# New places for the steps of a pipelined two-attention transformer on one Trainium2 core

## The reference

```
x = x + attn_a(layernorm(x))     # 16 heads of 16, window |i-j| <= 32 and 4 global tokens, biases
x = x + ffn(layernorm(x))        # silu(x wg) * (x wu) wd, 256 -> 768 -> 256, int32 weights / 127
x = x + attn_b(layernorm(x))     # rotated q, k; num = exp(q_rot k_rot), den = sum(exp(q k)), causal
x = x + ffn(layernorm(x))        # the same weights as before
```

## Time and profile before

| | us |
|---|---|
| median of 3 runs | 2082.86 (2078.55 to 2094.81) |
| the profiled execution | 2086.18 |
| its span | 2084.1 |
| mean granted clock of TensorE | 0.939 |

### The profile page before, as it was taken

One profiled execution on the slowest core, in us unless ns is written; L12 is line 12 of the kernel. 1 busy time (PEld: TensorE's weight loads), 2 busy tenths in 40 slices (PEclk: granted clock), 3 DMA queues, 4 the chain that ended last, 5 costly groups with the idle time before them and its releaser, 6 DMA issues.

```text
span 2084.1 us, 63373 instructions
## 1 busy us (share of the span) xinstructions
PE 1814.1 (87%) x25221; PEld 1137.5 (55%) x25221; DVE 1423.0 (68%) x2978; ACT 1436.6 (69%) x3591; POOL 789.0 (38%) x1140
## 2 busy tenths in 40 slices
PE   5577889999898999989899998989899998988785
PEld 3353556555564655556465555646555565655444
DVE  6373768677676867767686776768687676865634
ACT  2227777786867777686777768676776867677591
POOL 0513243433434343342434334243434424343431
PEclk7687999999999999999999999999999999998987
DMA  6223344243434424343442424343243435333321
GB/s 155 72 44 94 81 118 102 91 109 86 119 76 117 108 84 110 89 112 74 117 108 84 113 87 113 73 132 93 85 113 90 113 69 135 90 102 86 79 70 37
DMA packets 129204, 199.51 MB, mean 96 GB/s; under 512 B 26720, under 2 KB 60512, under 8 KB 128880
## 3 DMA queue, kind: packets, MB, share of 16 engines
q1 hardware_dynamic: 128912, 195.44, 37.1%
HBM read 67.87 MB, written 51.52 MB: 57 GB/s over the span
## 4 chain that ended last, share of the span: by engine, by line
PE 45%; ACT 20%; SPq 11%; DVE 9%; DMA 7%; issue 4%; POOL 3%; POOLq 0%; ACTq 0%; DVEq 0%
PE psum L1120 10%; SPq L634 8%; ACT psum L1236 8%; PE psum L1150 5%; ACT probs_B L1226 4%; PE psum L1138 4%; PE psum L1071 4%; PE psum L1017 4%; DMA pack_b<-src_b 4%; PE psum L1053 3%; SPq L667 3%; PE psum L1094 3%; ACT probs_A L1219 3%; PE psum L883 3%; PE psum L1084 3%
## 5 line engine op out<-in xcount | busy, mean ns | idle before, releaser
L1236 ACT ACTIVATE psum<-psum 128x512 f32<-128x512 f32 x1024 | 607.6, 604 | 118.0 <-PE psum L1017 116.5
L1659 POOL TENSOR_TENSOR h<-tmp,h 128x512 f16<-128x512 f32 x192 | 227.7, 1186 | 410.7 <-DVE h L1540 410.7
L1226 ACT ACTIVATE probs_B<-psum 128x512 f32<-128x512 f32 x640 | 333.3, 632 | 51.0 <-PE psum L1038 48.7
L1017 PE MATMUL psum<-pack_b 48*128 48x512 f16 x1024 | 181.7, 396 | 53.2 <-DMA pack_b<-src_b 31.9
L1120 PE MATMUL psum<-xT,w_g 128*128 128x256 f16 x1536 | 204.0, 276 | 13.4 <-ACT psum L1236 12.1
L1265 ACT ACTIVATE tmp<-psum 128x512 f32<-128x512 f32 x192 | 118.2, 616 | 138.4 <-PE psum L1120 125.7
L1676 POOL TENSOR_SCALAR_AFFINE_SELECT probs_B<-probs_B 128x256 f32<-128x256 f32 x512 | 194.0, 412 | 50.4 <-ACT probs_B L1226 50.4
L1236 ACT ACTIVATION_READ_ACCUMULATOR psum<-psum 128x1 f32 x1024 | 209.6, 205 | 0.0
L1120 PE MATMUL psum<-xT,w_u 128*128 128x256 f16 x1536 | 208.7, 276 | 0.0
L1138 PE MATMUL psum<-w_d,h 128*128 128x256 bf16 x1536 | 200.8, 274 | 8.3 <-POOL h L1659 7.1
L1523 DVE SCALAR_TENSOR_TENSOR tmp<-tmp,psum 128x512 f32<-128x512 f32 x192 | 130.2, 679 | 96.3 <-ACT tmp L1265 95.8
(11 more groups left out here) (150 smaller groups left out, 3210.5 us busy)
## 6 DMA issues: line engine op xcount, KB each, us to landing
pack_b<-src_b SPq DMA_DIRECT2D x768, 64.0 KB, 2.4
pack_a<-src_a SPq DMA_DIRECT2D x384, 64.0 KB, 2.3
x<-in_L_attn_a_x_dram SPq DMA_DIRECT2D x32, 512.0 KB, 4.2
o_scr_A<-o_raw SPq DMA_DIRECT2D x64, 256.0 KB, 2.5
o_scr_B<-o_raw SPq DMA_DIRECT2D x64, 256.0 KB, 2.4
xn<-o_scr_A SPq DMA_DIRECT2D x32, 256.0 KB
rden_on<-r_scr_A SPq DMA_DIRECT2D x32, 256.0 KB
x_scr<-x SPq DMA_DIRECT2D x16, 512.0 KB, 2.8
```

Of the source, the lines that this page charges most:

```text
L1017: pe.matmul(score_bank("DP", n, q, e)[:, :], pack_b[r, j % 2, 0, 0, tile, t * P:(t + 1) * P], pack_b[r, j % 2, 0, 1, tile, :], start=True, ...
L1226: act.activation(probs["B"][:, i, :], score_bank("NP", n // 2, q, n % 2)[:, :], ACT.Exp, scale=SM_SCALE / W_SCALE ** 2)\
L1236: act.activation(bank[:, :], bank[:, :], ACT.Exp, scale=SM_SCALE / W_SCALE ** 2, accum_out=den[:, 0, j, 2 * tile + e, t:t + 1]).then_inc(d ...
L1659: pool.tensor_tensor(h[1][:, i % 2, :], tmp[:, i % 2, :], h[0][:, i % 2, :], ALU.subtract)\
```

## The change

The table `AT` has other places, for nearly all of its steps; nothing else in the kernel is changed. No step is added, removed or cut otherwise, `TURN` stays 425, and the rule for the banks is the same code, which gives other banks for the other order. A place is now given to a hundredth. Most steps keep their neighbours. Those whose order changes on their engine, as far as the text speaks of them (a place minus a multiple of 425 gives the order within a turn):

```
-    "A2": (545.8, 551.7, 553.1, 557.2, 558, 585.3, 587.2, 621.2, 628.3),
+    "A2": (546.52, 548.28, 548.95, 549.16, 563.1, 582.22, 590.11, 617.03, 619.36),
-    "MM": (505.5,),
-    "TM": (528.9,),
-    "TC": (531.4,),
-    "MX": (533.4,),
+    "MM": (496.94,),
+    "TM": (509.76,),
+    "TC": (518.06,),
+    "MX": (435.36,),
-    "AT": (576.4, 623.7, 656.2, 677.7),
+    "AT": (582.57, 625.43, 655.69, 677.7),
-    "DP": (1052.2, 1060.5, 1065.8, 1067.3, 1074.8, 1080.7, 1085, 1090.9, 1093.8, 1112.3, 1124.1, 1125.2, 1134.4,
+    "DP": (1055.22, 1055.45, 1059.54, 1059.55, 1069.69, 1071.13, 1083.56, 1089.05, 1089.06, 1111.48, 1121.99,
...
-    "DE": (1057.1, 1066.7, 1070.3, 1074, 1080.6, 1084.2, 1087.8, 1092.4, 1096, 1115.3, 1126, 1129.7, 1135.9, 1141.9,
+    "DE": (1053.5, 1064.4, 1065.39, 1074.89, 1076.27, 1077.72, 1083.02, 1089.83, 1095.82, 1120.72, 1125.56, 1126.72,
...
-    "NE": (1102.1, 1104.9, 1107.8, 1118.9, 1121.8, 1153.4, 1158.4, 1162.3, 1168.9, 1219.3, 1307.6, 1311.6, 1318.8,
+    "NE": (1099.96, 1100.14, 1103.85, 1104, 1119.45, 1152.13, 1152.27, 1162.22, 1165.78, 1206.07, 1307.09, 1311.67,
...
-    "UL": (1035.3, 1058, 1106.2, 1222.7),
-    "RL": (1083.5, 1119.4, 1139, 1277),
-    "VB": (1054.5, 1061.5),
+    "UL": (1027.19, 1054.99, 1101.57, 1218.45),
+    "RL": (1056.62, 1109.32, 1128.13, 1277.55),
+    "VB": (1057.97, 1067.28),
-    "GL": (425.1,),
-    "SL": (361.2, 384.2, 395.8, 407.3),
+    "GL": (435.68,),
+    "SL": (381.05, 382.82, 385.25, 385.26),
-    "W": (1030.1, 1039.1, 1046.2, 1053.2),
-    "W1": (1036.6, 1041.4, 1050.5, 1055.3),
-    "W2": (1043, 1052.7, 1062.3, 1077.6),
+    "W": (1031.74, 1039.53, 1050.63, 1054.55),
+    "W1": (1032.7, 1039.42, 1050.96, 1054.89),
+    "W2": (1045.95, 1047.35, 1058.22, 1067.07),
-    "PBT2": (1020.8, 1024.9, 1028.9, 1033),
+    "PBT2": (1020.8, 1028.33, 1028.34, 1033.43),
-    "F1FD": (922.2, 948.2, 955, 965.1, 979.8, 985.8),
+    "F1FD": (922.22, 950.59, 954.04, 965.06, 977.17, 980.21),
```

More of the change, by code:

```diff
@@ L64 @@
 AT = {
[37 rows of a table removed]
[L102 to L105, removed]
-    "GL": (425.1,),
-    "SL": (361.2, 384.2, 395.8, 407.3),
-    "GB": (361.2,),
-    "W": (1030.1, 1039.1, 1046.2, 1053.2),
-    "W1": (1036.6, 1041.4, 1050.5, 1055.3),
-    "W2": (1043, 1052.7, 1062.3, 1077.6),
[L112 to L116, removed]
@@ L117 @@
-    "PBT2": (1020.8, 1024.9, 1028.9, 1033),
[L118 to L163, removed]
-    "F1X1": (898.9,),
[L165 to L172, removed]
@@ L173 @@
-    "F1J": (916.7, 933, 946.1, 953.2, 965.6, 973.8),
-    "F1JL": (918.2, 934.6, 947.6, 954.7, 967.2, 975.3),
-    "F1FD": (922.2, 948.2, 955, 965.1, 979.8, 985.8),
[L176 to L189, removed]
[37 rows of a table added]
+    "VBC": (1064.43, 1086.91),
+    "VA": (362.08, 390.23),
+    "VAC": (363.66, 391.38),
+    "GW": (419.32,),
+    "GL": (435.68,),
+    "SL": (381.05, 382.82, 385.25, 385.26),
+    "GB": (361.17,),
@@ new lines @@
+    "W": (1031.74, 1039.53, 1050.63, 1054.55),
+    "W1": (1032.7, 1039.42, 1050.96, 1054.89),
+    "W2": (1045.95, 1047.35, 1058.22, 1067.07),
+    "PAT": (329.19, 335.99, 340.68, 341.4),
+    "PAT1": (326.69, 343.97, 350.19, 350.69),
+    "PAT2": (334.37, 346.37, 354.24, 354.85),
+    "PBT": (1020.89, 1020.9, 1021.84, 1024.96),
+    "PBT1": (1009.38, 1009.39, 1014.21, 1022.05),
+    "PBT2": (1020.8, 1028.33, 1028.34, 1033.43),
+    "OAOR": (764.01,),
+    "OAOL": (740.64, 742.56),
+    "OAOM": (784.38, 785.17),
@@ new lines @@
+    "OAOH": (788.67, 811.98),
+    "OAOW": (811.19, 818.14),
+    "OAO": (834.24, 844.65),
+    "OAOX": (834.2, 843.29),
+    "OBOR": (1445.53,),
+    "OBOL": (1450.55, 1472.59),
+    "OBOM": (1466.95, 1490.31),
+    "OBOH": (1469.95, 1493.14),
+    "OBOW": (1476.04, 1498.47),
+    "OBO": (1506.04, 1512.17),
+    "OBOX": (1514.72, 1516.81),
+    "F2L0": (1518.94,),
+    "F2L1": (1519.78,),
+    "F2L2": (1528.16,),
+    "F2L3": (1528.6,),
+    "F2L4": (1529.9,),
+    "F2L5": (1530.14,),
+    "F1L0": (856.41,),
@@ new lines @@
+    "F1L1": (858.81,),
+    "F1L2": (875.41,),
+    "F1L3": (879.96,),
+    "F1L4": (880.09,),
+    "F1L5": (881.36,),
+    "PBL0": (992.38,),
+    "PBL1": (993.27,),
+    "PBL2": (1001.55,),
+    "PBL3": (1002.19,),
+    "PBL4": (1003.04,),
+    "PBL5": (1003.44,),
+    "NAL0": (257.16,),
+    "NAL1": (263.89,),
+    "NAL2": (281.28,),
+    "NAL3": (282.21,),
+    "NAL4": (282.75,),
+    "NAL5": (289.13,),
+    "PAX": (310.79,),
+    "PAXH": (305.1,),
+    "PAX1": (310.5,),
+    "F2X": (1532.2,),
@@ new lines @@
+    "F2XH": (1529.11,),
+    "F2X1": (1534.18,),
+    "F1X": (895.27,),
+    "F1XH": (896.84,),
+    "F1X1": (898.9,),
+    "PBX": (1005.54,),
+    "PBXH": (1004.91,),
+    "PBX1": (1011.99,),
+    "F1G": (906.49, 920.92, 921.44, 943.43, 947.46, 962.98),
+    "F1GT": (904.09, 922.67, 924.36, 940.75, 943.07, 962.76),
+    "F1U": (906.5, 922.86, 940.35, 945.47, 959.61, 967.78),
+    "F1H": (906.96, 923.61, 926.96, 948.86, 954.13, 963.77),
+    "F1I": (912, 927.57, 946.47, 950.65, 963.13, 968.27),
@@ new lines @@
+    "F1J": (913.05, 929.83, 947.58, 951.57, 967.33, 969.36),
+    "F1JL": (906.81, 934.81, 953.66, 957.1, 964.67, 968.39),
+    "F1FD": (922.22, 950.59, 954.04, 965.06, 977.17, 980.21),
+    "F1E": (954.77, 981.97),
+    "F2G": (1545.75, 1555.51, 1556.13, 1604.18, 1632.91, 1645.18),
+    "F2GT": (1546.01, 1559.36, 1563.11, 1604.39, 1636.03, 1637.16),
+    "F2U": (1546.58, 1583.59, 1593.26, 1614.25, 1652.36, 1662.6),
+    "F2H": (1550.35, 1563.81, 1573.89, 1612.12, 1639.65, 1653.71),
+    "F2I": (1550.55, 1585.28, 1604.9, 1617.89, 1656.06, 1663.93),
@@ L190 @@
+    "F2J": (1561.02, 1590.1, 1608.32, 1637.95, 1658.78, 1742.83),
+    "F2JL": (1561.57, 1575.46, 1587.99, 1636.74, 1682.13, 1734.23),
+    "F2FD": (1588.89, 1634.89, 1650.08, 1735.03, 1745.92, 1761.18),
+    "F2E": (1665.78, 1763.07),
+    "XL": (717.21,),
+    "BI": (725.47,),
+    "XS": (1775.82,),
+    "XA": (226.29,),
     "XO": (1018.5,),
-    "BP": (1009.9,),
-    "XB": (1429.9,),
+    "BP": (1010.51,),
+    "XB": (1429.86,),
 }
```

## The result

The changed kernel takes 2019.05 us (median of 4 runs, 2015.47 to 2025.06) against 2084.69 (2078.55 to 2094.81) for the one before in the same rounds: a ratio of 0.970, 95% interval 0.966 to 0.974, or 65.6 us less. The forecast was 2039, from terms that added up to a gain of 46.

What follows compares the result with a forecast made beforehand. PE's work plus its waits was taken as the bound: 109.91 us busy in a 120 us turn. Terms summed to 3.1 us a turn, 46 us in 15 turns, 2082.9 to 2037, stated as 2039; range 2010 to 2079.

Steps and rivals of the forecast that it cites:

- Items 1 and 2: Maxima earlier (TM, MM, TC, MX); FD4 and FD5 of F1 earlier: X of PB starts 1.0 us earlier a turn.
- the slower rival: MX at the head of SyncE's queue delays GL, so PE stands at AV0: 2122 us, chance 0.09.
- Items 3 and 4: First packs of B and rotated packs, from X of PB to NE0: a gain of 2.6 us a turn.
- the last sentence of the forecast: Likeliest error: the sum holds, and PE stands at X of F2 or G0 of F2 for what NP0 gained.
- half is given back: Rival: PE arrives early at X of F2 and stands for DVE; 1.2 us a turn, 2065 us, chance 0.12.
- Item 5: ACT's long stretch behind NP0, with NE3 ahead of XH of F2: taken as nothing.
- item 4: DP1 right behind DP0 on PE, W2.3 behind DE2 on ACT: NP0's 2.24 us wait goes, but for some 0.2.
- Item 6: Fewer changes of array split in PE's order, 0.09 us each: 0.35 us a turn, 0.15 left to count.
- Item 7: Packs of A, UL3 issued ahead of SL0: 0.2 us a turn; A1.5's wait of 0.7 stays.
- Item 8: All other new places on DVE, GpSimd and SyncE, and new bank waits: a loss of 0.7 us a turn.
- item 1: Maxima's steps and transfers earlier on PE, DVE, ACT and SyncE: A2.1's wait of 0.42 us goes.
- The clock: PE's clock falls behind long waits; not in the sum, up to 1.5 us a turn, held by the low end.

Runs made afterwards that it cites:

- e4_both: Kernel before with the edits of Items 1 and 2 and Items 3 and 4 together: 0.994 of before, 13 us less.
- e2_rot_early: Kernel before with Items 3 and 4 alone on PE and ACT, W1.0 left in place: 0.996 of before, 7.5 us less.
- run 10: e10_np3_late: kernel after with NP3 put back behind DP9 on PE, NE3 and NE4 behind DE9 on ACT: 2028.17 us, 0.972 of before.
- e9_np3: e4_both with NP3 ahead of X of F2 on PE, NE3 and NE4 ahead of DE9 on ACT: 2059.46 us, 0.987 of before.
- e11_np3_banks: e9_np3 with the bank rule also steered at three steps, NP6, AV0 and X of PA: 2051.20 us, 0.983 of before.
- run 12: Kernel after with eleven swaps of neighbours undone on PE alone: 2056.15 us, 0.984 of before.
- runs 5 and 6: Kernel before with PE's places from the kernel after: 2110.26 us, 1.010; kernel after with PE's places from the kernel before: 2140.54 us, 1.024.
- e6_others: Kernel after with all PE steps at the places of the kernel before: 2140.54 us, 1.024 of before.
- e8_bv1_first: Kernel after with A1.3 behind BV1 on PE and AM3 behind BT1 on DVE, as before: 2025.94 us, 0.969 of before.

## Why the prediction was right, and where its sum was wrong

The sign and the range were right, and what it said that the profile would show: a turn of 117.5 (116.25), no wait at A2.1, NP0's wait under 0.5 (0.1 on average), GpSimd's under 1 (0.76), X of PB 0.9 (1.1, but for a bank in place of xn), DP0 1.3 (1.2). The size was 20 us short, and the sum reached even that by luck in part: of its 3.1 us a turn, items 1 to 4 carried some 3.5, and on the chip those items alone give 0.9. (The sum gives 2037; no term stands for the 2 us up to 2039.)

*Items 1 and 2.* Alone 10 us, forecast 15: right within the interval. The stretch from E1 of F1 to X of PB, which I held fixed at 5.16, is 5.51: X stands for a bank that NE17 empties (963.12), and the first part of xn is ready at nearly the same time. GL had 3.6 us to spare at AV0 (958.70, less 951.81 and 3.3), forecast 2.3; the slower rival never came near.

*Items 3 and 4.* From X of PB to NE0 2.6 us were forecast; the means of eleven turns are 34.10 and 32.05, so 2.05. The turn that I read was one in which the clock falls behind X of PB (X of PB to NE0 35.9 there, 34.1 on average), which should have been seen by reading all turns. That is the smaller error. The larger is that this gain was put in the sum in full. In e4_both and e2_rot_early it exists and is mostly not kept, as the last sentence of the forecast had it: PE stands at X of F2 (1.75 us a turn in e4_both, 0.54 before) for what it gained at NP0. The clock took a part as well: in e4_both it is at half speed for 8.4 us a turn, 7.1 before. For these items alone the rival "half is given back" was nearer than the forecast (0.9 us a turn, its 1.2, the forecast's 3.5).

*Item 5*, "nothing", was wrong beside items 1 to 4: with NE3 and NP3 ahead of X of F2 the stretch behind NP0 is 1.2 us shorter and the time 15 us less than with those items alone. In the kernel after, undoing the same pair costs 6 us, which its interval doesn't tell from nothing (run 10). So it is one way to keep the gain of item 4, and not shown to be the only one.

*Item 6.* Not confirmed. e4_both, e9_np3 and e11_np3_banks have 1219 changes of split, fewer than the 1223 of the kernel after, and are 32 to 53 us slower by the medians; run 12 has 13 more, which by 0.09 is 1.2 us, and costs 30. Changes of split went along with good neighbours and aren't what pays. PE's busy time of a turn is 0.95 us less. Of that some 0.3 is the clock, an estimate: half of the 0.6 us less that it is at half speed (7.1 and 6.5 us a turn, from the two traces). The rest isn't divided.

*Item 7.* A1.5's 0.67 us is gone, against "stays", but PE has 0.66 us of idle time in the stretch from T3 of PA to X of F1, in place of 0.70: O0 of OA stands 0.40 for DVE. The reason, DVE without a gap, was right, and the place of the wait wasn't.

*Item 8*, the rest, was taken as a loss of 0.7 us a turn and is the mis-sized term. PE's idle time falls by 0.47 us from G0 to FD0 of F2, by 0.87 from X of F1 to A2.1 and by 0.39 from there to X of PB, and item 1 explains only the 0.42 at A2.1, a part of the second. Run 12 shows that such moves are worth as much as that: eleven swaps of neighbours on PE, which the forecast priced nowhere but as changes of split (item 6), cost 30 us when put back. It doesn't show that they are the missing term. Its waits are at other steps than those of e11_np3_banks, which stands 0.76 us a turn at AV2, 0.68 at A1.5, 0.41 at DP6 and 0.31 each at NP7 and X of PA; only X of PA is common to both. And it is itself half of an order put back, as runs 5 and 6 were, which can cost more than the whole gives. What the four waits of run 12 do show is that the forecast's rule, a step passed by a few short ones costs nothing if its data is there, left out the step's bank.

*The clock* was left out of the sum. Before and after it is at half speed for the same 103 us between 200 and 1900 us of the span (7.1 and 6.5 us a turn), so it doesn't explain the 66. But it is a term of the same size as most experiments' effects: 78 us in e9_np3, 120 in e4_both, 137 in e6_others.

What stays open: the 28 to 32 us between e11_np3_banks and the kernel after (by the ratios, by the medians). That the orders of DVE, GpSimd and SyncE carry it, with the banks that go with them, is a rival that no run here excludes. Run 12 says that PE's neighbours carry about that much inside the new order; which of the eleven, and with which step of ACT or DVE each belongs, wasn't tried. No version here beats the kernel after; e8_bv1_first and e10_np3_late can't be told from it.

## What to carry to other kernels

An order written out for several engines belongs together: PE's half of a good one, or the rest without PE's, was slower than the old one, while a few moves chosen across engines gave a part of the gain (13 us, then 28, then 36 of 66). Price a chain that gets shorter only up to the next step at which the fast engine must stand, here X of F2, three steps behind NP0 in the old order, and look there for the move that keeps the gain before you count it. Small moves of neighbours are not noise when buffers are handed out by the same order; sum the waits of 0.3 to 0.9 us in every stretch, for all turns and not one. When you undo a move to price it, look whether the waits that appear are those that the move was to explain: in run 12 the size fitted and the places did not.

## What the runs showed of the hardware

The clock falls to half behind waits of 1 to 2 us that come once or twice a turn, and whether it does varies from turn to turn. X of PB and the two quarters behind it, in two turns of the kernel after, windows with the granted clock third from the end:

```profile
963.12:965.51 2.39, 2.39 (x48) 1.47 (x48) 2.39 (x6) 2.32 (x5) 1.84 (x4) 1.00 0.02 3
1078.45:1082.02 3.57, 3.57 (x49) 2.22 (x49) 3.57 (x7) 2.43 (x5) 3.02 (x6) 0.59 0.02 5
```

The same work takes 1.2 us longer where the clock is mostly at 1.2 GHz than where it is at 2.4, in the chain that sets DP0, and the wait ahead of X was the same (1.05 and 1.06 us). Of the table's eleven turns it fell so in 8 after and in 4 before (T0 of PB starts over 3 us behind X there, and 2.2 to 2.4 in the others). The longest idle time in these turns is 2.47 us before and 1.86 after. The Trainium skill, "TensorE: Matmul & The Clock Gate", HAM oscillation, ties the fall to idle gaps longer than any in these turns.

In the kernel after the cast of OH0 of OB (L1458) took 1.38 us beside GpSimd's second sum (L1664), and the same cast of OH1, with no GpSimd work beside it, 0.43. The first ended 0.29 us behind the sum. In the kernel before the cast of 1.40 us ended 0.28 us behind the GpSimd difference beside it, and 33 casts with GpSimd idle took 0.41 to 0.43. So the forecast's measure for it, a product's 0.68, made the loss too small: it is some 0.95 us. The sum took 1.73 us, where the fourth took 1.27.
